# A decoder's opening: parameter rows on a second DMA queue, constants after roots, token mixing folded into the weights

## The chip, the cores and the metric

The kernel runs on one core of a Trainium2 chip. The metric is the device time of one execution in microseconds (us), lower is better. A core has a matrix engine (TensorE, PE in the rows), a vector engine (VectorE, DVE), an activation engine (ScalarE, ACT), a general engine (GpSimd, POOL) and a sync engine (SyncE, SP) whose work here is to issue DMAs. Each engine runs its own instruction list in order, and they meet only at semaphores.

## The reference

Two decoder layers are computed over x (8 sequences of 256 tokens, width 128) with a context of 8 x 512 tokens. Six sublayers follow each other, each followed by a layer norm of x plus the sublayer: a recurrent block (RWKV), memory attention, a top-1 mixture of experts, sparse attention, cross attention, and a top-2 mixture. Only the first matters for this change:

```python
h = layer_norm(x, ln_att_g, ln_att_b)
sx = time_shift(h)                       # h of the token before, 0 ahead of the first
k = (h * att_mix_k + sx * (1.0 - att_mix_k)) @ att_wk
v = (h * att_mix_v + sx * (1.0 - att_mix_v)) @ att_wv
r = sigmoid((h * att_mix_r + sx * (1.0 - att_mix_r)) @ att_wr)
att = r * wkv(att_time_decay, att_time_first, k, v) @ att_wo   # a recurrence over tokens
x = x + att
h = layer_norm(x, ln_ffn_g, ln_ffn_b)
sx = time_shift(h)
kf = square(relu((h * ffn_mix_k + sx * (1.0 - ffn_mix_k)) @ ffn_wk))
rf = sigmoid((h * ffn_mix_r + sx * (1.0 - ffn_mix_r)) @ ffn_wr)
return x + rf * (kf @ ffn_wv)
```

`wkv` keeps a running maximum of the keys that decays by `w` per token, a numerator and a denominator, both scaled by exponentials of differences to that maximum, and divides the one by the other.

## The kernel before

The batch is worked in 4 groups of 2 sequences, 512 tokens each. The recurrent block of group n + 1 is computed inside the last two sublayers of group n, beside their matmuls. For group 0 there is nothing to put it beside: it stands alone at the start, with the loading and turning of the weights. This stretch is called the opening, and the change touches it alone. After it come the four groups.

Everything is ordered by hand: each engine's block is a Python function that emits its instructions in order, and waits are written as `wait_ge(semaphore, count)`. There is no planner.

**The loads.** SyncE issues all DMAs of the opening. First x of group 0, then `rec_loads`: 12 single rows of 128 parameters (layer norm scales, decay, mixes) and 6 blocks of rows into the tile `col_rows`, then wk, wv, wr, wo, fwk, fwv, fwr. Then `loads` (weights of the attentions, 4 of them of 512 KB into the arena's `xw_raw`, and 8 rows for broadcasts), the context, and `layer_loads` (expert weights).

**TensorE** waits for GpSimd's constants (`consts_ready`, line 531) and for all of `rec_loads` (line 532). Then it turns `col_rows` (78 rows) into `cols`, whose columns hold one parameter per partition (`set_up(0)`, line 516), turns the normalised x (line 479), and multiplies the three mixed inputs by wk, wv and wr (line 556). After the wait for `weights_loaded` it turns 8 groups of four 128 x 128 weight blocks and two more weights; then `rec_attend` (the product with wo, line 499), which waits for VectorE's `wkv_ready`; then `qk_fold` (line 518), the sum `xbv_out` (16 instructions, line 523), 8 rows broadcast over the partitions by a matmul with ones (line 527); after all of those have been copied, the turn of the context (line 539), two key projections of 128 x 512 (`project_k`, line 760), the turn of the second normalised input, two value projections (`project_v`, line 766), and the feed forward matmuls (line 567 on). An fp32 product shows as two instructions in the trace.

**ScalarE** copies results out of the accumulator banks (line 1127), applies scale and shift to the turned input (line 1159, tile `hT`), and computes the exponentials (lines 1171, 1173) and the sigmoid (line 1177). In the opening it holds back after `set_up(0)` until `cols_ready` is 6, that is until VectorE has derived five small tables from `cols`.

**GpSimd** first makes all constants: memsets, iotas, selects (line 1461), copies (lines 1473, 1474). Then come the two reciprocal square roots of the first layer norm (`rec_rstd`, lines 1491 and 1493), the two products `b2v` and `bv_` (lines 1534, 1538), the three steps of the numerator `t_num` (lines 1542, 1544, 1549), the roots of the second norm, and the split of the expert bias b1 into three bf16 parts (lines 1624 to 1630).

**VectorE** computes the norm's moments and the normalised x (lines 1652 to 1660), the token change `dT` (line 1684) and the three mixes (line 1690, two instructions each), the running maximum (a scan for each sequence, line 1720), the own maximum (line 1726), four differences (line 1735), the denominator's scans (line 1740) and the numerator's (line 1745), two steps of `t_den` (lines 1752, 1754), reciprocals (line 1758), and the product with GpSimd's numerator (line 1763). This last gives `wkv_ready`.

The listing holds the functions that the diff touches. Names of tiles are reused in the trace: `big` is `ex` or a product, `nT` the keys, `V` the values, `arena` any tile carved from it.

## Time and profile before

| what | value |
|---|---|
| median of 3 runs | 1188.58 us |
| lowest, highest | 1184.47, 1196.2 us |
| the profiled execution | 1197.25 us |
| its span in the trace | 1195.5 us |
| busy: PE, PEld, DVE, ACT, POOL | 1063.4, 661.9, 726.5, 646.6, 186.0 us |

The profiled execution is one run of its own: its time is the span and 1.75 us around it, and it lies 8.67 us above the median of the three runs. Durations of steps come from its trace, so sums are made against 1197.25. PE is the matmul side of TensorE, PEld its loading of weights, which overlaps. The busy time of PE is not PE at its peak, since matmuls are pipelined. Lines such as L1740 are lines of the kernel before.

### The profile page before, as it was taken

The page shows a single profiled execution, that of the slowest core. Times are in us where ns is not written, and L with a number is a line of the kernel's source. Part 1 is how long each engine was busy: PE and PEld are TensorE (multiplying, and loading weights), DVE is VectorE, ACT ScalarE, POOL GpSimd, SP SyncE. Part 2 cuts the span into 40 slices and gives each one's busy share as a digit, 9 for nine tenths or more (in the row PEclk, how much of TensorE's full clock was granted, in tenths as well). Part 3 has the DMA queues.
Part 4 walks back from the last instruction along what each step waited for, and adds up shares of the span by engine and source line. Part 5 has one row for each costly group of instructions (what it writes and reads, how often), then busy time and mean ns, then how long its engine had stood idle before and what let it go on. Part 6 is the DMA issues. An engine that isn't in the chain of part 4 may idle for free.

```text
span 1195.5 us, 23126 instructions
## 1 busy us (share of the span) xinstructions
PE 1063.4 (89%) x8821; PEld 661.9 (55%) x8821; DVE 726.5 (61%) x1827; ACT 646.6 (54%) x1429; POOL 186.0 (16%) x313
## 2 busy tenths in 40 slices
PE   3789988998989998999898998899979999899957
PEld 1664545554766456455586454555567635545546
DVE  5552475888644175788854338488874417567861
ACT  3452356775655054778565235577755605477724
POOL 4320220212120040012102013020212004000000
PEclk9799999999899998999899999999989999899979
DMA  7400000000000000000000000000000000000000
GB/s 221 143 1 1 1 2 4 8 19 2 2 11 1 1 1 1 10 20 2 1 1 11 1 1 1 2 10 19 1 1 10 1 1 1 2 1 2 2 1 10
DMA packets 21072, 15.77 MB, mean 13 GB/s; under 512 B 871, under 2 KB 18644, under 8 KB 20956
## 3 DMA queue, kind: packets, MB, share of 16 engines
q1 hardware_dynamic: 20956, 14.24, 4.0%
q8 instruction: 70, 1.15, 0.4%
q14 instruction: 46, 0.38, 0.1%
HBM read 13.18 MB, written 1.05 MB: 12 GB/s over the span
## 4 chain that ended last, share of the span: by engine, by line
PE 41%; issue 40%; ACT 5%; POOL 5%; DVE 5%; POOLq 1%; DVEq 1%; SPq 1%; DMA 0%; ACTq 0%
PE ps L728 10%; PE ps L908 5%; PE ps L944 4%; PE ps L926 3%; PE ps L760 3%; PE ps L766 3%; POOL rstd L1493 2%; PE ps L757 2%; ACT arena L1328 2%; PE ps L627 1%; PE ps L953 1%; PE ps L741 1%; DVE nmax L1982 1%; ACT arena L1127 1%; PE ps L660 1%
## 5 line engine op out<-in xcount | busy, mean ns | idle before, releaser
L1127 ACT ACTIVATE arena<-ps 128x512 f32<-128x512 f32 (+6 forms) x300 | 162.9, 575 | 146.2 <-PE ps L926 56.2
L1328 ACT ACTIVATE arena<-ps,nmax 128x512 f32<-128x512 f32 x256 | 173.6, 685 | 7.9 <-DVE nmax L1982 4.8
L1982 DVE TENSOR_REDUCE nmax<-ps 128x1 f32<-128x512 f32 x256 | 163.9, 683 | 22.6 <-PE ps L908 22.0
L1987 DVE COPY arena<-ps 128x512 f32<-128x512 f32 x128 | 88.1, 688 | 61.0 <-PE ps L926 61.0
L926 PEld LDWEIGHTS ps<-ident,arena 64*128 64x128 f32 x2048 | 76.6, 138 | 82.7 <-issue 42.2
L728 PE MATMUL ps<-big,w1a 128*128 128x512 f32 x256 | 117.3, 604 | 0.0
L926 PE MATMUL ps<-ident,arena 64*128 64x64 f32 x2048 | 92.4, 228 | 11.7 <-ACT arena L1127 6.3
L1491 POOL TENSOR_TENSOR vare<-mv,eps_ln 128x2 f32<-128x2 f32 x64 | 13.0, 204 | 565.8 <-DVE mv L1655 565.5
L728 PEld LDWEIGHTS ps<-big,w1a 128*128 128x128 f32 x256 | 46.3, 189 | 57.5 <-issue 56.5
L1875 DVE TENSOR_TENSOR big<-XT,ps 128x512 f32<-128x512 f32 x32 | 22.0, 687 | 90.4 <-PE ps L712 90.3
L1991 DVE SCALAR_TENSOR_TENSOR X<-ps,cross_inv,X 128x128 f32<-128x128 f32 x256 | 72.4, 342 | 3.2 <-issue 0.5
L1270 ACT ACTIVATE big<-ps 128x512 f32<-128x512 f32 x16 | 9.6, 597 | 116.1 <-PE ps L728 116.1
L760 PE MATMUL ps<-ctxT,xwT 128*128 128x512 f32 x128 | 68.8, 653 | 0.0
L766 PEld LDWEIGHTS ps<-xwT,ctxT 128*128 128x128 f32 x512 | 62.3, 193 | 8.1 <-issue 7.7
L766 PE MATMUL ps<-xwT,ctxT 128*128 128x128 f32 x512 | 65.0, 278 | 0.0
L1493 POOL TENSOR_TENSOR rstd<-vare,neg_half 128x2 f32<-128x2 f32 x72 | 51.1, 710 | 10.2
L1328 ACT ACTIVATION_READ_ACCUMULATOR arena<-ps,nmax 128x1 f32 x256 | 51.6, 202 | 0.0
L953 PEld LDWEIGHTS ps<-xwT,arena 64*128 64x128 f32 x512 | 31.6, 187 | 20.5 <-DVE arena L1987 16.8
L1915 DVE TENSOR_TENSOR arena<-ps,s_nmax 128x1024 f32<-128x1024 f32 x32 | 39.2, 1225 | 2.4
L1908 DVE TENSOR_REDUCE s_nmax<-ps 128x8 f32<-128x1024 f32 x32 | 38.9, 1216 | 1.9 <-PE ps L818 1.9
L831 PEld LDWEIGHTS ps<-ident,arena 64*128 64x128 f32 x512 | 19.5, 146 | 36.7 <-ACT arena L1291 30.2
L953 PE MATMUL ps<-xwT,arena 64*128 64x128 f32 x512 | 38.0, 285 | 1.9 <-ACT arena L1127 1.9
(376 smaller groups left out, 2035.4 us busy)
## 6 DMA issues: line engine op xcount, KB each, us to landing
ctx<-in_ctx_dram SPq DMA_DIRECT2D x4, 512.0 KB, 3.9
w1a<-in_L_ffn_W_dram SPq DMA_DIRECT2D x1, 2048.0 KB, 9.6
w1b<-in_L_ffn_W_dram SPq DMA_DIRECT2D x1, 2048.0 KB, 11.6
w2b<-in_L_ffn_W_dram SPq DMA_DIRECT2D x8, 256.0 KB, 6.9
X<-in_x_dram SPq DMA_DIRECT2D x4, 256.0 KB, 2.8
out_dram<-Y SPq DMA_DIRECT2D x4, 256.0 KB, 2.3
arena<-in_L_xattn_Wq_dram SPq DMA_DIRECT2D x1, 512.0 KB
arena<-in_L_xattn_Wk_dram SPq DMA_DIRECT2D x1, 512.0 KB
```

What stands on the lines that cost most here:

```text
L728: last = pe.matmul(bank(acc[h]), w1a[:, e, h * P:(h + 1) * P], XE[:, e % 2, :], start=(e == 0), stop=(e == E - 1))
L760: pe.matmul(bank(b), xwT[:, 1, j, :], ctxT[:, seq * CTX:(seq + 1) * CTX], start=True, stop=True)\
L766: last = pe.matmul(ps[:, b, k * P:(k + 1) * P], ctxT[:, c * P:(c + 1) * P], xwT[:, 2, j, :], start=True, stop=True)
L908: pe.matmul(bank(2 * (t % 2) + h), QTs[r, j % 2, t * P:(t + 1) * P], keys_of(j, t // QT)[r, :], start=True, stop=True).then_inc(c_ps, 1)
L926: last = pe.transpose(ps[:, 4 + u, o:o + DK], cprob[r, 2 * (t % 2) + h, k * P:(k + 1) * P], ident[r, r])
L953: last = pe.matmul(ps[:, b + h, t * D:(t + 1) * D], CTs[r, j % 2, t * P:(t + 1) * P], xwT[r, 3, j, :], start=True, stop=True)
L1127: return act.activation(dst, src, ACT.Copy)
L1328: act.activation(cprob[:, 2 * (t % 2) + h, :], bank(2 * (t % 2) + h), ACT.Exp, bias=nmax[:, s:s + 1], accum_out=rsum[:, j % 2, s:s + 1]).t ...
L1493: return pool.tensor_tensor(result[:, r], with_eps[:, r], neg_half[:, r], ALU.pow)
L1982: dve.tensor_reduce(nmax[:, s:s + 1], bank(s % 4), AX.X, ALU.max, negate=True)\
L1987: dve.tensor_copy(cprobT[:, 2 * (t % 2), :], bank(4)).then_inc(cT_even, 1)
L1991: last = dve.scalar_tensor_tensor(out=X1[:, t, :], in0=ps[:, b, t * D:(t + 1) * D], scalar=cross_inv[:, j % 2, 2 * t + h:2 * t + h + 1], i ...
```

## The change

- The 12 single parameter rows (`first_rows`) are issued by ScalarE's queue; SyncE issues x, then wk, wv, wr (`mix_loads`), then the rest as before. TensorE's first work waits for the identity matrix and the 12 rows alone.
- GpSimd makes the identity and the small constants first, signals `ident_ready`, makes some more, then does the first norm's roots. The masks come after the roots, the head constants after the numerator, the expert rows (`pick`) after the second norm's roots; `consts_ready` is awaited at the end of the opening.
- `col_rows` is turned in two parts: the 12 rows first, all else later as `set_up(1)`.
- The token change and the three mixes of the opening are gone. VectorE splits each weight instead, `own = w * mix` and `past = w - own`, and TensorE forms h @ own + sx @ past: two products instead of one. The keys are computed a sequence at a time, and ScalarE's copies and VectorE's scans too.
- ScalarE no longer waits for `cols_ready` 6 ahead of `hT`; that wait now stands before the turned context. Three of the five small tables are made after `wkv_ready`.
- VectorE computes `b2v` and `bv_`; GpSimd waits for `den_ready`, the finished denominator, and then computes the three steps of the numerator.
- `qk_fold` comes before `rec_attend`; the broadcast rows before `xbv_out`; the second turn after one key projection instead of two.
- In the four groups no instruction changes.

```diff
-            pe.wait_ge(consts_ready, 1)
-            pe.wait_ge(rec_loaded, 16 * len(rec_loads))
+            pe.wait_ge(ident_ready, 1)
+            pe.wait_ge(rows_loaded, 16 * len(first_rows))
             set_up(0)
...
+            def first_turn():
+                pe.wait_ge(xhat_ready, 1)
+                turn_seq(NHAT, 5, 0).then_inc(half_turned, 1)
+                pe.wait_ge(xhat_ready, 2)
+                turn_seq(NHAT, 4, 1).then_inc(hT_ps, 1)
+
+            def first_keys(seq):
+                if seq == 0:
+                    pe.wait_ge(half_ready, 1)
+                    pe.wait_ge(mix_ready, 1)
+                else:
+                    pe.wait_ge(hT_ready, 1)
+                o = ps[:, 6 + seq, seq * SEQ:(seq + 1) * SEQ]
+                pe.matmul(o, own_w[0], hT[:, seq, 1:SEQ + 1], start=True, stop=False)
+                return pe.matmul(o, past_w[0], hT[:, seq, 0:SEQ], start=False, stop=True)
+
+            def first_project(w, b):
+                pe.wait_ge(vr_mix_ready, w)
+                pe.matmul(bank(b), own_w[w], hT[:, :, 1:SEQ + 1], start=True, stop=False)
+                pe.matmul(bank(b), past_w[w], hT[:, :, 0:SEQ], start=False, stop=True).then_inc(kvr_ps, 1)
+
             def first_recurrent(n):
-                rec_turn(n, 1, 5)
-                rec_project(n, 0, 6)
-                rec_project(n, 1, 7)
-                rec_project(n, 2, 5)
+                first_turn()
+                first_keys(0).then_inc(half_key_ps, 1)
+                first_keys(1).then_inc(kvr_ps, 1)
+                first_project(1, 5)
+                first_project(2, 4)
+                pe.wait_ge(rec_loaded, 16 * len(rec_loads))
+                set_up(1)
 
                 pe.wait_ge(weights_loaded, 16 * len(loads))
-                for i in range(1, N_TURNS):
+                for i in range(2, N_TURNS + 1):
                     set_up(i)
                 rec_attend(n)
-                for i in range(N_TURNS, N_SETUP):
+                for i in range(N_TURNS + 1, N_SETUP):
                     set_up(i)
                 pe.wait_ge(wT_sb, N_SETUP)
                 turn_ctx(n, 2)
-                for seq in range(GROUP):
-                    pe.wait_ge(ctxT_ready, n * 2 + seq + 1)
-                    project_k(5, seq, seq)
+                pe.wait_ge(ctxT_ready, n * 2 + 1)
+                project_k(5, 0, 0)
                 rec_turn(n, 2, 5)
+                pe.wait_ge(ctxT_ready, n * 2 + 2)
+                project_k(5, 1, 1)
                 for seq in range(GROUP):
                     project_v(5, 2 + seq, seq)
                 for h in range(HT):
@@ -605,6 +638,7 @@
                 rec_gate(n)
                 rec_narrow(n, 0)
                 rec_narrow(n, 1)
+                pe.wait_ge(consts_ready, 1)
 
...
+            for dst, src in first_rows:
+                act.dma_start(dst, src).then_inc(rows_loaded, 16)
             set_up(0)
             act.wait_ge(wT_sb, 1)
             act.activation(decay_e[:, :], col(R_DECAY), ACT.Exp).then_inc(cols_ready, 1)
-            act.wait_ge(cols_ready, 6)
...
             def first_recurrent(n):
-                rec_turned(n, 1, 5, R_LNG, R_LNB)
-                rec_projected(n, 0, 6)
-                rec_projected(n, 1, 7)
-                for i in range(4):
-                    rec_exp(n, i)
-                rec_receptance(n, 5)
+                act.wait_ge(half_turned, 1)
+                first_turned(0).then_inc(half_ready, 1)
+                act.wait_ge(hT_ps, 1)
+                first_turned(1).then_inc(hT_ready, 1)
+                act.wait_ge(half_key_ps, 1)
+                first_key(0).then_inc(half_key_ready, 1)
+                act.wait_ge(kvr_ps, 1)
+                first_key(1).then_inc(kvr_ready, 1)
+                rec_exp(n, 0)
+                rec_exp(n, 1)
+                rec_projected(n, 1, 5)
+                rec_exp(n, 2)
+                rec_exp(n, 3)
+                rec_receptance(n, 4)
                 for i in range(1, N_SETUP):
                     set_up(i)
+                act.wait_ge(cols_ready, 6)
                 ctx_turned(n, 2)
-                for seq in range(GROUP):
-                    keys(n, 5, seq, seq)
+                keys(n, 5, 0, 0)
                 rec_turned(n, 2, 5, R_FLNG, R_FLNB)
+                keys(n, 5, 1, 1)
                 for seq in range(GROUP):
                     context_values(n, 5, 2 + seq, seq)
```

On GpSimd and VectorE (bodies of `masks`, `head_constants` and `expert_rows` are the old instructions, regrouped):

```diff
             pool.memset(ident[:, :], 0.0)
-            pool.memset(causal_f[:, :], 0.0)
...
             pool.memset(neg_half[:, :], -0.5)
             pool.memset(eps_ln[:, :], 1e-5)
             pool.memset(eps_rms[:, :], 1e-6)
             pool.memset(eps_post[:, :], 1e-12)
+            pool.memset(ones[:, :], 1.0)
+            pool.drain()
+            select(ident[:, :], ALU.not_equal, 1.0, 0, [[-1, P]], 1)
+            pool.drain().then_inc(ident_ready, 1)
+            pool.memset(causal_f[:, :], 0.0)
+            pool.memset(before_f[:, :], 1.0)
...
@@ -1613,11 +1672,13 @@
                 rstd_of(it, 6, eps_ln)
 
             rec_rstd(0, 1)
-            rec_weighted_values(0)
-            rec_own_values(0)
+            masks()
+            pool.wait_ge(den_ready, 1)
             rec_numerator(0)
             rec_numerator_gated(0)
+            head_constants()
             rec_rstd(0, 2)
+            expert_rows()
 
             pool.wait_ge(b1_loaded, 16)
...
+            def mixed_weights(w, row, done):
+                dve.tensor_scalar(own_w[w], (wk, wv, wr)[w][:, :], col(row), None, ALU.mult)
+                dve.drain()
+                dve.tensor_tensor(past_w[w], (wk, wv, wr)[w][:, :], own_w[w], ALU.subtract).then_inc(done, 1)
+
+            def first_difference(i, a, b):
+                dve.tensor_tensor(ex[i][:, :, :], a, b, ALU.subtract).then_inc(wkv_arg, 1)
+
+            def first_max(b):
+                return dve.tensor_tensor_scan(o_max[:, b, 1:SEQ + 1], w_bc[:, :], kS[:, b, :], -1e38, ALU.add, ALU.max)
+
+            def first_columns():
+                dve.wait_ge(cols_ready, 1)
+                dve.wait_ge(mix_loaded, 16 * len(mix_loads))
+                mixed_weights(0, R_MK, mix_ready)
+                dve.tensor_scalar(decay_w[:, :], decay_e[:, :], -1.0, None, ALU.mult).then_inc(cols_ready, 1)
+                mixed_weights(1, R_MV, vr_mix_ready)
+                dve.tensor_scalar(w_bc[:, :], w_bc[:, :], decay_w[:, 0:1], None, ALU.add).then_inc(cols_ready, 1)
+                mixed_weights(2, R_MR, vr_mix_ready)
...
+            def first_recurrent(n):
+                dve.wait_ge(half_key_ready, 1)
+                first_max(0)
+                dve.wait_ge(kvr_ready, 1)
+                first_max(1).then_inc(o_max_ready, 1)
+                dve.drain()
+                first_difference(0, o_max[:, :, 0:SEQ], o_max[:, :, 1:SEQ + 1])
+                first_difference(1, kS[:, :, :], o_max[:, :, 1:SEQ + 1])
                 rec_first_max()
                 dve.drain()
-                rec_differences()
+                first_difference(2, o_max[:, :, 0:SEQ], o_new[:, :, :])
+                first_difference(3, kS[:, :, :], o_new[:, :, :])
                 rec_key_sum(n)
+                dve.wait_ge(kvr_ready, 2)
+                dve.tensor_tensor(b2v[:, :, :], ex[1][:, :, :], vS[:, :, :], ALU.mult).then_inc(b2v_ready, 1)
                 rec_value_sum(n)
+                dve.wait_ge(wkv_exp, 4)
+                dve.tensor_tensor(bv_[:, :, :], ex[3][:, :, :], vS[:, :, :], ALU.mult)
                 rec_denominator(n)
+                dve.drain().then_inc(den_ready, 1)
                 for b in range(GROUP):
                     rec_inverse(b)
                 rec_wkv(n)
+                other_columns()
                 rec_second_norm(n)
                 rec_feed_mix(n)
                 rec_feed(n)
```

## Rows read from the trace of the kernel before

**Rows 1.** The page: the span, and the chain that ended last, by engine.

```profile
span 1195.5 us, 23126 instructions
...
PE 41%; issue 40%; ACT 5%; POOL 5%; DVE 5%; POOLq 1%; DVEq 1%; SPq 1%; DMA 0%; ACTq 0%
...
```

**Rows 2.** Windows: stretch, busy us (count) by engine, granted clock, DMA, GB/s.

```profile
...
66.00:1195.00 1129.00, 1026.56 (x8645) 634.80 (x8643) 689.00 (x1741) 621.75 (x1376) 158.68 (x244) 0.97 0.02 4
28.40:31.50 3.10, 2.88 (x14) 2.88 (x15) 3.01 (x4) 2.74 (x7) 1.43 (x2) 0.51 1.10 350
35.40:42.00 6.60, 4.41 (x20) 4.41 (x21) 3.99 (x10) 0.28 (x1) 0.52 (x2) 0.50 1.21 296
45.50:48.50 3.00, 3.00 (x10) 1.73 (x8) 0.00 (x0) 1.20 (x2) 2.59 (x4) 0.50 0.00 0
...
```

**Rows 3.** Chain of waits, opening: start, duration (us), what was waited for.

```profile
...
9.75 3.05 DMA fwr<-in_L_attn_ffn_wr_dram
...
13.84 0.15 DVE decay_w L2148
...
17.83 2.09 PE ps L556 x2
...
```

**Rows 4.** Timeline of SyncE's DMA issues: start, duration (us), destination, source.

```profile
...
0.82 0.45 SPq L440 DMA_DIRECT2D X<-in_x_dram  x1
...
4.68 0.25 SPq L451 DMA_DIRECT2D col_rows<-in_L_xattn_norm_w_dram  x1
...
18.63 0.25 SPq L453 DMA_DIRECT2D arena<-in_L_ffn_br_dram  x1
...
25.59 13.65 SPq L457 DMA_DIRECT2D w2b<-in_L_ffn_W_dram  x8
...
```

**Rows 5.** Timeline of VectorE, opening; in brackets idle time before, releaser.

```profile
...
10.50 0.60 DVE L1660 TENSOR_SCALAR NHAT<-X,mv,rstd 128x128 f32<-128x128 f32 x2 [5.39 <-POOL rstd L1493]
...
20.57 1.27 DVE L1720 TENSOR_TENSOR_SCAN o_max<-w_bc,nT 128x256 f32<-128x256 f32 x2 [1.22 <-ACT nT L1127]
...
25.33 3.36 DVE L1740 TENSOR_TENSOR_SCAN q_den<-big 128x256 f32<-128x256 f32 x2
...
29.95 1.71 DVE L1752 TENSOR_TENSOR big<-big,q_den 128x512 f32<-128x512 f32 x1
...
33.41 3.36 DVE L1758 RECIPROCAL alpha<-big 128x256 f32<-128x256 f32 x2
...
43.67 0.85 DVE L1660 TENSOR_SCALAR NHAT<-X,mv,rstd 128x128 f32<-128x128 f32 x2 [0.66 <-POOL rstd L1493]
...
```

**Rows 6.** Timeline of GpSimd, opening.

```profile
...
9.41 0.19 POOL L1491 TENSOR_TENSOR vare<-mv,eps_ln 128x2 f32<-128x2 f32 x1
...
24.96 1.57 POOL L1534 TENSOR_TENSOR big<-big,V 128x512 f32<-128x512 f32 x1 [13.50 <-ACT big L1173]
...
```

**Rows 7.** Timeline of TensorE, opening.

```profile
...
22.83 1.97 PE L516 MATMUL ps<-ident,arena 128*128 128x128 f32 x16 [0.30 <-DMA arena<-in_L_ffn_br_dram]
...
37.59 2.08 PE L499 MATMUL ps<-wo,alpha 128*128 128x128 f32 x8 [5.19 <-DVE alpha L1763]
...
49.95 1.95 PE L766 MATMUL ps<-xwT,ctxT 128*128 128x128 f32 x16
52.81 3.70 PE L567 MATMUL ps<-qT,fwk 128*128 128x512 f32 x8 [0.91 <-DVE qT L1690]
...
61.60 1.88 PE L760 MATMUL ps<-ctxT,xwT 128*128 128x512 f32 x4
...
```

**Rows 8.** Groups by form, VectorE after 60 us: count, busy us, mean ns.

```profile
...
L1752 DVE TENSOR_TENSOR big<-big,q_den 128x512 f32<-128x512 f32 x3 | 2.1, 693 | 0.5 <-issue 0.5
...
```

**Rows 9.** Groups by form, GpSimd after 60 us; idle before.

```profile
...
L1549 POOL TENSOR_TENSOR big<-big,OT 128x512 f32<-128x512 f32 x3 | 3.8, 1266 | 11.4 <-ACT OT L1177 11.4
...
```

**Rows 10.** Timeline of ScalarE, opening.

```profile
...
26.18 1.28 ACT L1177 ACT_TABLE_LOAD   x1
...
27.97 3.25 ACT L1127 ACTIVATE xwT<-ps 128x512 f32<-128x512 f32 x6
...
```

137 lines of the change are left out of this document (67 added, 70 removed).

## The prediction

> **What bounds the kernel now.** I read the page first, then windows of the opening, then the chain of waits, then each engine's timeline. The page's chain belongs to TensorE and to issue time [rows 1]. After 66 us TensorE is busy 1026.56 of 1129.00 us at a granted clock of 0.97, and no instruction of that stretch changes [rows 2]. So what the opening loses or gains arrives at the end nearly one for one, and the rest stays as it is. The other windows of [rows 2] matter for the clock: three stretches stood at 0.5 (1.2 of 2.4 GHz).
>
> In the opening the chain of waits goes from SyncE's list of DMA issues to the landing of fwr at 12.80, by the small tables to the first mix, and to the key product at 17.83 [rows 3]. After it VectorE is the chain, up to the product that releases TensorE at 37.59. From there TensorE leads, until the feed forward at 52.81 and the first layer's end.
>
> **The change part by part.** All sums are against this execution, 1197.25 us with 1195.5 us of span.
>
> Start of the key product. x is issued at 0.82 and the last single row at 4.68; with x's 0.45 taken off, the 12 rows cost about 0.3 each [rows 4]. ScalarE can start its own list when SyncE does, so its last issue begins at 0.82 + 11 x 0.3 = 4.1. A load with others ahead of it took 3.05 from issue to landing (fwr, [rows 3]), so the rows are there at 7.2 at the latest; a little less is likely for 0.5 KB, I take 7.0. From landing to VectorE's first small table took 1.04 (12.80 to 13.84); 12 columns instead of 78 make it 0.9. The split of wk is one scalar product and one subtraction on 128 x 128, about 0.7 with the drain. The first key product starts at 8.6 instead of 17.83: **-9.2** (ends: -9.6, rows at 6.6; -6.7, issues at twice the price on that queue).
> What could be later is the normalised x. VectorE had its moments ready at 10.50 - 5.39 = 5.11 and waited for GpSimd's roots, which stood behind the constants until 9.41 [rows 5, 6]. A root takes 1.09 from its start to x (9.41 to 10.50). With fewer constants ahead it follows the moments: x is there at 6.2 and 7.2, beside the wait for the rows, and costs nothing. If GpSimd got to it only at 7, the second half would come at 9.1 and hold the second key product alone, which starts later than that.
>
> Keys. Before, product, copy and both scans took 17.83 to 20.57 + 1.27 = 21.84, so 4.0. The product was two instructions of 512 columns in 2.09, and the same form took 1.88 / 4 = 0.47 each at 61.60 [rows 7]: it ran at half speed though the record there shows no lower clock. Now there are eight of 256 columns, as long as four of 512: 4 x 0.95 = 3.8. The first half's copy and scan lie beside the second half's product, the second half's cost 1.1. 4.9 against 4.0: **+0.9** (ends: -1.0 at full speed; +1.5).
> The doubled products for v and r are needed only by `b2v` and by the numerator's last step; 2 x 3.8 after the keys end at about 21, beside VectorE's maximum and differences. `b2v` needs only v, at 16.
>
> From the scans to the reciprocals. The denominator's two scans took 3.36, the same form 1.27 [rows 5], the first with GpSimd's product of 1.57 beside it [rows 6]: -2.1. The two steps of `t_den` took from 29.95 to 33.41, 3.46, beside the numerator; alone such a step takes 0.69 [rows 8], 1.5 with drains: -1.9. VectorE takes over `b2v` and `bv_`, 2 x 0.69: +1.4. Two more waits: +0.2. Together **-2.4** (ends -1.6 and -2.8).
> The rows show VectorE slowed by 2.1 and 1.9 beside GpSimd's products; the numerator beside the reciprocals is the price to watch. The Trainium skill (SBUF — State Buffer, "Who interferes with whom") says that the two engines share one pair of ports exclusively, a VectorE operation with two SBUF inputs against a GpSimd one that reads; by it the reciprocals, with one input, are free. The trace agrees as far as it goes: 3.36 for two, next to GpSimd's last step.
>
> Numerator. All three steps now start after the denominator, beside the reciprocals (3.36). Alone a step took 1.27 [rows 9], three with drains 4.1 and the semaphore 0.1; at 1.57 each 5.0. So the product waits 0.8 to 1.7 more than before; I take **+0.9**.
>
> Masks. GpSimd makes them from about 7 on, beside VectorE's splits. NHAT beside a GpSimd cast took 0.85 where the same pair took 0.60 [rows 5]. Two or three such hits: **+0.2** (0 to +0.9).
>
> The release of TensorE (T) thus moves by -9.2 + 0.9 - 2.4 + 0.9 + 0.2 = -9.6, from 37.59 to 28.0. Is all else there by then? The last small row was issued at 18.63 and TensorE waited for it until 22.83 [rows 4, 7]. 12 issues leave SyncE's list, 3.6: landing at 19.2. ScalarE's table load of 1.28 before the sigmoid and then the weight copies, 3.25 for six [rows 10], ten copies 5.2: done at 25. The cover is 3 us. Were the loads bound by transfer, not issue, they would land at 22.83 and the copies end at 28.2: +0.2. `qk_fold` slips into this gap, two of L499's eight at 2.08: **-0.4** (0 to -0.5) [rows 7].
>
> Second turn. One projection, two instructions of 512 columns (0.94), moves behind the turn. TensorE was idle for 0.91 before 52.81, after value projections of 1.95 [rows 7]; the chain turn, ScalarE, VectorE now begins 0.94 earlier and TensorE has 2.9 of work under it. Gain 0.9 at most. But GpSimd's expert rows and split of b1 now lie beside VectorE's change and mixes, all of two inputs; the scans lost 2.1 to such a neighbour. **0** (-0.9 to +1.2).
>
> Clock. Before, TensorE was idle 5.19 ahead of 37.59 and the clock stood at 0.50 from 35.4 to 42.0, with 4.41 us of work: half of it, 2.2, is lost; from 45.5 to 48.5 another 1.5. At 28.4 to 31.5 the clock was low too, after an idle stretch, and rose while TensorE only turned weights [rows 2]. Now the idle gap before T is 3 at most, perhaps 2, with the turned weights right before it. Either the clock holds (-2.2) or it doesn't; and the weak work of the broadcast rows now lies just before `xbv_out`, so a low stretch after it costs up to +1.5. **-0.8**.
>
> Sum: -9.6 (to T) - 0.4 + 0 - 0.8 = **-10.8**. The profiled time becomes 1186.4. The median of the runs stands 8.67 below the profiled one, so I forecast 1188.58 - 10.8 = **1177.8 us**, 0.91% less.
>
> **The rivals.** What a measurement can tell from no change is about 1%, 11.9 us.
>
> *The clock holds through the opening.* -2.2 in place of -0.8, no block at the second turn (-0.9), the keys partly at full speed (-0.8): -10.8 - 1.4 - 0.9 - 0.8 = -13.9, with some of it -12. Time 1174.7 to 1176.6. For: the shorter gap. Against: the key product ran at half speed and its idle lead-in stays.
>
> *GpSimd's moved work blocks VectorE.* Numerator +1.7, masks +0.9, second turn +1.2: 2.7 more than forecast, -8.1: 1180.5. For: NHAT's 0.85, the scans' 3.36. Against: much of it is small, on 8 partitions.
> By the rule of the Trainium skill named above this would be the way it goes, for the split of b1 reads SBUF throughout.
>
> *The rows land late.* Both queues feed the same engines; at twice the price of an issue the last begins at 7.4, the key product at 12: -7.5, so 1181.
>
> *The expected gain isn't there*, because a later load or wait ends last. The expert weights were issued until 39.24 [rows 4], and no load of the opening is on the chain after 22.83. I see no such wait.
>
> *Slower.* One mechanism: ScalarE's queue comes under back-pressure. SyncE's eight issues of w2b took 13.65, 1.7 each [rows 4]. At that price the 12 rows begin their last issue at 19.5 and land at 22.5, 15.5 later than forecast: -10.8 + 15.5 = +4.7, 1193. It decides from 1.3 per issue on, and the kernel is slower by over 1% from 2.4 on (22.7 / 11 more than 0.3). Against: it came behind megabytes in the queue, and here only x and small weights are under way.
>
> **How the numbers follow.** Forecast, -9 to -12: 0.48, of which 0.07 lies beyond 1%. Clock holds, -12 to -14: 0.32. GpSimd blocks: 0.08. Rows late: 0.04. No gain: 0.02. Slower: 0.06, of which 0.04 by over 1%. So faster by over 1%: 0.07 + 0.32 = 0.39; within 1%: 0.41 + 0.08 + 0.04 + 0.02 + 0.02 = 0.57; slower: 0.04. The likeliest time is 1177.8. The range reaches from the clock's case, 1174.7, to the late rows, 1181, and gets 4 more at each end because medians stray (three runs lie between 1184.47 and 1196.2): 1171 to 1185. It leaves out the slower case, no gain, and the tails.
>
> **What would show it.** The wait for the 12 rows ends at 7.0 and the first key instruction starts at 8.6; later by more than 1 means the queue. The denominator's scans take 1.27, each `t_den` step 0.69; more means GpSimd is still beside them. GpSimd's three steps end 0.9 after the reciprocals. T is at 28.0. The set-up copies end before T, or the loads did not move up. The second mixes at the feed forward take 0.48 each, or b1's split is in their way. The granted clock around T is 1.0 in the rival and 0.5 in the forecast's worse half. The stretch after the first layer lasts as long as before. The forecast is wrong if T lies above 31, or if the later groups change their length by over 3 us.

## The result and the profile after

The changed kernel takes 1178.14 us (median of 15 runs, 1176.0 to 1188.04), the kernel before 1190.68 us (median of 15, 1184.47 to 1197.71). The ratio is 0.9894, with a 95% interval of [0.9872, 0.9915]: 12.5 us or 1.06% less. The forecast was 1177.8. Its size was 10.8; the kernel before came out 2.1 higher than in the first three runs, so part of the agreement of the two absolute times is luck: the change is worth 1.7 more than forecast, and the kernel that it is taken from is 2.1 slower.

The profiled execution after took 1182.05 us, with a span of 1180.1. So it is 15.2 us shorter than the one before [rows 1], and both lie above their medians. The page after, the chain by engine (before: [rows 1]):

```profile
...
issue 42%; PE 41%; POOL 6%; ACT 5%; DVE 4%; POOLq 2%; DVEq 1%; ACTq 0%; DMA 0%
...
```

TensorE still owns the end; the share of SP's queue is gone from the chain. Windows of the kernel after, with columns as in [rows 2] (behind the counts of the five engines stands the granted clock):

```profile
...
17.70:24.30 6.60, 5.60 (x26) 5.60 (x27) 6.25 (x8) 4.58 (x9) 2.45 (x2) 0.51 0.99 336
24.70:42.00 17.30, 14.89 (x90) 11.02 (x89) 11.74 (x26) 9.30 (x25) 13.35 (x27) 1.00 0.96 284
...
```

One stretch of low clock is left, while the weights are turned; from 24.7 on the clock stood at 1.0 where before two more stretches were at 0.5 [rows 2]. Now the timeline of TensorE after (start, duration; in brackets the idle time before it and what ended it):

```profile
...
6.79 0.25 PE L524 MATMUL ps<-ident,col_rows 12*128 12x12 f32 x1 [6.79 <-DMA col_rows<-in_L_xattn_norm_w_dram]
...
8.40 1.19 PE L604 MATMUL ps<-hT,kv_more 128*128 128x256 f32 x2 [0.32 <-ACT hT L1223]
...
11.04 0.59 PE L605 MATMUL ps<-hT,kv_more 128*128 128x256 f32 x2
...
18.70 6.59 PE L524 MATMUL ps<-ident,arena 128*128 128x128 f32 x32 [3.56 <-DMA arena<-in_L_ffn_br_dram]
...
26.49 1.16 PE L507 MATMUL ps<-wo,alpha 128*128 128x128 f32 x8 [0.46 <-DVE alpha L1813]
...
38.76 3.70 PE L575 MATMUL ps<-qT,fwk 128*128 128x512 f32 x8 [1.26 <-DVE qT L1751]
...
43.87 3.84 PE L587 MATMUL ps<-fwv,big 128*128 128x128 f32 x32 [0.52 <-DVE big L1832]
...
```

The 12 rows are there at 6.79, the keys start at 8.40 instead of 17.83, the weights land at 18.70 instead of 22.83, and T, the release of TensorE, comes at 26.49 instead of 37.59 [rows 3, 7]. The idle time ahead of it fell from 5.19 to 0.46 in this execution. VectorE and GpSimd after:

```profile
...
5.59 0.60 DVE L1721 TENSOR_SCALAR NHAT<-X,mv,rstd 128x128 f32<-128x128 f32 x2 [0.48 <-POOL rstd L1552]
...
12.09 0.69 DVE L1854 TENSOR_TENSOR_SCAN o_max<-w_bc,nT 128x256 f32<-128x256 f32 x1 [0.50 <-ACT nT L1161]
...
16.26 1.27 DVE L1790 TENSOR_TENSOR_SCAN q_den<-big 128x256 f32<-128x256 f32 x2
...
20.08 0.69 DVE L1802 TENSOR_TENSOR big<-big,q_den 128x512 f32<-128x512 f32 x1
...
21.70 3.37 DVE L1808 RECIPROCAL alpha<-big 128x256 f32<-128x256 f32 x2 [0.16 <-issue]
25.75 0.69 DVE L1813 TENSOR_TENSOR alpha<-alpha,big 128x512 f32<-128x512 f32 x1 [0.68 <-POOL big L1608]
...
36.63 2.08 DVE L1751 SCALAR_TENSOR_TENSOR qT<-O,cols,hT 128x256 f32<-128x256 f32 x2
38.63 2.23 DVE L1751 SCALAR_TENSOR_TENSOR qpT<-O,cols,hT 128x256 f32<-128x256 f32 x2
...
```

```profile
...
4.50 0.20 POOL L1550 TENSOR_TENSOR vare<-mv,eps_ln 128x2 f32<-128x2 f32 x1 [1.48 <-DVE mv L1716]
...
24.44 1.27 POOL L1608 TENSOR_TENSOR big<-big,OT 128x512 f32<-128x512 f32 x1
...
36.16 1.51 POOL L1689 TENSOR_TENSOR arena<-arena 8x512 f32<-8x512 f32 x1
...
```

The denominator's scans take 1.27 instead of 3.36 and the first step of `t_den` 0.69 instead of 1.71 [rows 5]. The reciprocals keep their 3.37 with GpSimd's three steps beside them, and the product waits 0.68 for the last of these. Where GpSimd splits b1, the two mixes at the feed forward (two instructions each) take 2.08 and 2.23; alone such a mix takes 0.88.

**A second profile of each.** Both kernels were profiled once more, unchanged, in the last two experiments. In the tables below "first key" is the start of the first key product, "scans" the end of the maximum's two scans, "T" the start of the product with wo, "output" the start of the first feed forward output product (L579 before, L587 after).

| profile | first key | scans | reciprocals | T | output | span less output |
|---|---|---|---|---|---|---|
| before | 17.83 | 21.84 | 33.41 | 37.59 | 57.92 | 1137.6 |
| before, again | 18.66 | 22.68 | 34.24 | 38.42 | 58.53 | 1129.5 |
| after | 8.40 | 12.78 | 21.70 | 26.49 | 43.87 | 1136.2 |
| after, again | 8.56 | 13.47 | 22.39 | 27.16 | 48.72 | 1127.6 |

T repeats within 0.83 us for the same kernel, and moved by 11.1 and 11.3. What follows it does not repeat: 17.38 and 21.56 us from T to the output product for one and the same program, and 8 us more or less in the stretch after it.

### The profile page after: what moved, and what is told of

The parts are those of the page before. It is cut to its first block, busy times and chain, and to the rows that moved or that the text cites. A ratio compares the mean times of both kernels' runs of the same rounds, so it can differ in the third digit from the quotient of the medians.

```text
span 1180.1 us, 23157 instructions
## 1 busy us (share of the span) xinstructions
PE 1062.5 (90%) x8832; PEld 661.6 (56%) x8832; DVE 724.9 (61%) x1828; ACT 647.2 (55%) x1432; POOL 183.9 (16%) x311
## 2 busy tenths in 40 slices
DMA packets 21069, 15.74 MB, mean 13 GB/s; under 512 B 871, under 2 KB 18644, under 8 KB 20956
## 4 chain that ended last, share of the span: by engine, by line
issue 42%; PE 41%; POOL 6%; ACT 5%; DVE 4%; POOLq 2%; DVEq 1%; ACTq 0%; DMA 0%
PE ps L762 10%; PE ps L942 5%; PE ps L978 4%; PE ps L960 3%; PE ps L800 3%; PE ps L794 3%; POOL rstd L1552 2%; PE ps L791 2%; ACT arena L1379 2%; PE ps L987 1%; PE ps L775 1%; DVE nmax L2067 1%; PE ps L661 1%; ACT arena L1161 1%; POOLq L1551 1%
## 5 line engine op out<-in xcount | busy, mean ns | idle before, releaser
L865 PEld LDWEIGHTS ps<-ident,arena 64*128 64x128 f32 x512 | 19.2, 143 | 36.7 <-ACT arena L1342 30.1
```

## The experiments

My theory was the forecast's: T moves by the sum of its terms, and the total moves with T. The rivals that were left after the result: that the clock gives a part of the gain, that the second queue gives nothing, and that b1's split takes something back at the feed forward. Ten kernels change a part, two repeat a kernel unchanged; line numbers in their rows are their own.

### Rows issued by SyncE

```diff
-            for dst, src in first_rows:
-                act.dma_start(dst, src).then_inc(rows_loaded, 16)
...
             load_x(0)
+            for dst, src in first_rows:
+                sp.dma_start(dst, src).then_inc(rows_loaded, 16)
             for dst, src in mix_loads:
```

> The changed kernel, but SyncE issues the 12 single rows, after x and before wk, wv and wr, as before the change. Landmarks of the changed kernel: first key instruction at 8.40, release of TensorE by VectorE's last product (T) at 26.49, first feed forward output product at 43.87. If the second queue earns by its issue time (my theory): the rows land near 7.2 instead of 6.65, wk, wv and wr land 12 x 0.3 = 3.6 later, at 8 to 9, so the split of wk and the first key instruction come at 9 to 10; the loads for the weight turns land at 22.3 instead of 18.7, the turns (7 us) and copies end near 29.5 and T's work starts there, 3 later than now; output product at 46.5 to 47.5. If only the narrower wait earned (TensorE waits for 12 rows, not for all): first key instruction within 0.7 of 8.4 and T within 1 of 26.5.

Measured: 1177.52 us in one run, T 28.42, output 45.69: between the two cases that I had set out. TensorE and VectorE in its opening:

```profile
...
6.00 0.25 PE L526 MATMUL ps<-ident,col_rows 12*128 12x12 f32 x1 [6.00 <-DMA col_rows<-in_L_xattn_norm_w_dram]
...
22.19 5.54 PE L526 MATMUL ps<-ident,arena 128*128 128x128 f32 x32 [6.26 <-DMA arena<-in_L_ffn_br_dram]
...
28.42 1.06 PE L509 MATMUL ps<-wo,alpha 128*128 128x128 f32 x8
...
```

```profile
...
26.50 0.69 DVE L1813 TENSOR_TENSOR alpha<-alpha,big 128x512 f32<-128x512 f32 x1 [0.68 <-POOL big L1608]
...
```

The rows came earlier (6.00), not later. The wk, wv and wr behind them came later, but their split ended in time: first key 8.63, only 0.2 behind. What the 12 issues cost is the landing of the weights, 22.19 instead of 18.70. VectorE's product was done at 27.19, and TensorE, still with the turned weights and the fold of qk, came to it at 28.42. T is 1.3 to 1.9 later than in the two profiles of the kernel after. So ScalarE's queue is worth 1.2 us here (28.42 less 27.19), and through the later weights; VectorE's path gains 0.2 of it at most. The rest of the 1.9 lies mostly in the second half of the keys, which ran at half speed here as in the second profile of the kernel after.

### The roots behind all constants

```diff
-            rec_rstd(0, 1)
             masks()
+            head_constants()
+            expert_rows()
+            rec_rstd(0, 1)
             pool.wait_ge(den_ready, 1)
```

> The changed kernel, but GpSimd makes all its constants (masks, head constants, expert rows) before the first two roots. My prediction held that the roots must come early or the normalised x is late: roots at 9.4, x at 10.5 and 11.5, first key instruction at 12 instead of 8.40, T at 30 instead of 26.49. Rival: the rows and the split of the weights hold the keys anyway, and T moves by under 1. The output product then starts at 47 to 47.5 (theory) or below 45 (rival).

Measured: 1182.85 us in one run; first key 14.03, scans 18.81, T 32.49. GpSimd, and then TensorE:

```profile
...
10.29 0.18 POOL L1550 TENSOR_TENSOR vare<-mv,eps_ln 128x2 f32<-128x2 f32 x1
...
```

```profile
...
32.49 2.08 PE L507 MATMUL ps<-wo,alpha 128*128 128x128 f32 x8 [3.36 <-DVE alpha L1813]
...
```

The root starts 5.8 later and T is 5.3 to 6.0 later than in the two profiles of the kernel after. I had expected 3.5. VectorE's list splits wk only behind both halves of x, and the second half was normalised at 13.32, so the first key came at 14.03 and not at 12. This is the largest single part. The roots are worth it only since the 12 rows no longer hold the keys: before, the first half of x was normalised at 11.10 and TensorE's first work waited for fwr until 12.80 [rows 3, 5].

### The products and the numerator on GpSimd, as before

```diff
-            pool.wait_ge(den_ready, 1)
+            pool.wait_ge(kvr_ready, 2)
+            rec_weighted_values(0)
+            rec_own_values(0)
             rec_numerator(0)
...
-                dve.tensor_tensor(b2v[:, :, :], ex[1][:, :, :], vS[:, :, :], ALU.mult).then_inc(b2v_ready, 1)
...
-                dve.tensor_tensor(bv_[:, :, :], ex[3][:, :, :], vS[:, :, :], ALU.mult)
```

> The changed kernel, but GpSimd computes b2v, bv_ and the numerator as soon as their inputs are there, beside VectorE's sums, as before the change. Theory of the shared ports: the denominator's two scans take about 3.4 instead of 1.27 and the two t_den steps 3.4 instead of 1.5; VectorE is spared 1.35 for the two products and the numerator no longer trails the reciprocals (0.7): T later by 2 to 2.5, at 28.5 to 29. Rival, that VectorE was slow for another reason of the old order (the four differences, the exponentials on ScalarE): scans stay at 1.27, T is 1.5 to 2 earlier by VectorE, and held at 26 by the copies of the turned weights.

Measured: 1188.07 us in one run; scans 13.44, T 29.20. VectorE:

```profile
...
18.00 1.26 DVE L1792 TENSOR_TENSOR_SCAN q_den<-big 128x256 f32<-128x256 f32 x2
19.18 2.27 DVE L1797 TENSOR_TENSOR_SCAN p_num<-big 128x256 f32<-128x256 f32 x2
21.55 1.71 DVE L1804 TENSOR_TENSOR big<-big,q_den 128x512 f32<-128x512 f32 x1
...
```

The `q_den` scans, for which I had expected 3.4, escaped GpSimd's product here: it started at 16.07 and met the last difference instead (1.75 against 0.68). `p_num`'s scans and the steps of `t_den` did not escape (2.27, 1.71 and 1.61). The stretch from the scans to T is the number that repeats best. It lasts 15.75 and 15.74 in the two profiles of the kernel before and 15.76 here; with the products on VectorE it lasts 13.71 and 13.69 in the two after, 13.68 with the late roots and 13.70 with mixed inputs (below). So this part is worth 2.05 us at T, where the forecast had 1.5 (-2.4 + 0.9). (The kernel with the rows on SyncE is left out: TensorE and not VectorE sets its T.)

### Inputs mixed, weights not split

> The changed kernel, but the weights are not split: VectorE computes the token change and the three mixes of the inputs (0.69 + 3 x 0.88) and TensorE multiplies once, the keys still by sequence. Theory: hT is complete at 8.72, change and key mix end at 10.4, so the keys start 2 later, but take half as long (1.9 instead of 3.2); then the v and r mixes hold VectorE until 12.2. Maximum's end 13.5 to 14 instead of 12.78; T 27.2 to 27.8 instead of 26.49: the split earns about 1. Rival: it earns the whole time of change and mix, 1.6 to 2.4, and T is above 28.

```diff
-                mixed_weights(0, R_MK, mix_ready)
...
-                mixed_weights(1, R_MV, vr_mix_ready)
...
-                mixed_weights(2, R_MR, vr_mix_ready)
+                dve.wait_ge(hT_ready, 1)
+                token_change()
+                token_shift(zk, R_MK, mix_ready)
+                token_shift(zv, R_MV, vr_mix_ready)
+                token_shift(zr, R_MR, vr_mix_ready)
```

TensorE has one product for each of k, v and r again. Measured: 1177.92 us in one run; first key 10.75, scans 13.97, T 27.67. TensorE:

```profile
...
10.75 2.08 PE L601 MATMUL ps<-qT,wk 128*128 128x256 f32 x4 [2.36 <-DVE qT L1747]
...
```

The first key is 2.2 to 2.4 later, but with one product instead of two the keys take 3.2 instead of 4.4 to 4.9. What the split weights bring at T is 0.5 to 1.2.

### TensorE kept busy ahead of T, in the kernel before

```diff
                 for i in range(1, N_TURNS):
                     set_up(i)
+                for _ in range(5):
+                    pe.matmul(bank(6), wk[:, :], zk[:, :, :], start=True, stop=True)
                 rec_attend(n)
```

> The kernel before, with five products of 128 x 512 into a free bank put between the last turned weight and the product with wo: TensorE stays busy from 32.4 until 36.8 instead of idling 5.19; the five results are not used. Clock theory: from the release by VectorE's last product (T, 37.59) to the first feed forward output product took 20.33 there and 17.38 in the changed kernel, because the clock stood at 0.5 after the idle stretch. Here the granted clock stays at 1.0 around T, the product with wo takes 1.05 instead of 2.08, and the distance falls to 17.5 to 18.8 with T unchanged; the whole kernel gains 1.5 to 3. Rival, that the new order (broadcast rows first, second turn sooner) made the 17.38: the distance stays at 20.3 and the time is the same.

Measured: 1192.34 us median of 10 runs, ratio to before 0.9997 [0.9965, 1.0029]. The profiled execution:

```profile
...
31.68 5.17 PE L593 MATMUL ps<-qT,wk 128*128 128x512 f32 x10
37.42 1.16 PE L499 MATMUL ps<-wo,alpha 128*128 128x128 f32 x8 [0.57 <-DVE alpha L1765]
...
55.62 3.84 PE L579 MATMUL ps<-fwv,big 128*128 128x128 f32 x32 [0.52 <-DVE big L1784]
...
```

The clock held: the product with wo took 1.16 instead of 2.08 [rows 7], and T to output took 18.20 instead of 20.33. The opening is 2.3 to 2.9 shorter than in the two profiles of before, and the median of the total did not fall. But the interval reaches from 4.2 us less to 3.5 us more: it holds the whole gain of 2.3 to 2.9 as well as none. This run shows what the clock does to the opening, and leaves open whether the gain arrives at the end.

### b1 split behind the mixes

```diff
             expert_rows()
+            pool.wait_ge(mix_ready, 3)
 
             pool.wait_ge(b1_loaded, 16)
```

> The changed kernel, but GpSimd begins the split of b1 only after VectorE's last mix of the second turn. In the changed kernel the first mix took 2.09 instead of 0.88 and TensorE idled 1.26 ahead of the feed forward. Port theory: the change and mixes take 0.69 and 0.88 each, the feed forward starts right behind the value projections, at 37.6 to 37.8 instead of 38.76, output product at 42.7 to 42.9 instead of 43.87: the kernel gains 1.1. Rival: the mixes were slow for ScalarE's copies or the projections' reads; nothing moves.

Measured: 1179.06 us median of 8, ratio 0.9906 [0.9872, 0.994]. VectorE and TensorE at the feed forward:

```profile
...
36.47 0.88 DVE L1752 SCALAR_TENSOR_TENSOR qT<-O,cols,hT 128x256 f32<-128x256 f32 x2
...
39.19 4.60 DVE L1833 TENSOR_TENSOR big<-big 128x512 f32<-128x512 f32 x4 [1.05 <-ACT big L1216]
...
```

```profile
...
37.40 3.70 PE L575 MATMUL ps<-qT,fwk 128*128 128x512 f32 x8
...
43.84 5.46 PE L587 MATMUL ps<-fwv,big 128*128 128x128 f32 x32 [1.85 <-DVE big L1833]
49.14 1.88 PE L794 MATMUL ps<-ctxT,xwT 128*128 128x512 f32 x4
...
```

The mixes are free again (0.88) and the feed forward starts 1.36 sooner, without a wait. But now the split lies beside the squares, which need 4.60 for four, and the output product starts at 43.84 as in the kernel after. It then takes 5.46 instead of 3.84: TensorE had been idle for 1.85 and its granted clock was 0.69 on average from 43.84 to 49.30. The next projection starts at 49.14, in the kernel after at 47.55. So the cost was moved, not removed, and in this profile the late split loses 1.6 behind the landmark that I measured by.

### The second turn behind both key projections

> The changed kernel, but both key projections stand ahead of the second turn, as before the change. Forecast of the changed kernel: the sooner turn earns 0.9 unless GpSimd's split of b1 eats it; TensorE idled 1.26 behind it, so VectorE's chain is the bound there. Theory: turn, mixes and feed forward all come 0.9 later, from T to the output product 18.3 instead of 17.4 at the same clock. Rival: VectorE's mixes then fall past the split of b1, run at 0.88, and 0.5 or more of the 0.9 comes back.

```diff
                 project_k(5, 0, 0)
-                rec_turn(n, 2, 5)
                 pe.wait_ge(ctxT_ready, n * 2 + 2)
                 project_k(5, 1, 1)
+                rec_turn(n, 2, 5)
```

ScalarE's list follows it. Measured: 1187.27 us in one run; T 26.91. The feed forward:

```profile
...
42.02 5.40 PE L575 MATMUL ps<-qT,fwk 128*128 128x512 f32 x8 [2.53 <-DVE qT L1751]
...
```

The idle time ahead of it is 2.53 us instead of 1.26 (1.17 in the second profile of the kernel after). So the sooner turn is worth some 1.3, where I had said 0. It is one execution, and VectorE's change and first mix lay beside the split of b1 here too (1.13 and 2.07), while the second mix took 0.87. (Another 1.6 of the delay is the sum xbv_out at low clock, 3.61 instead of 2.05.)

### Unused products and the rows ahead of T

> The changed kernel, with b1's split late, four unused products of 128 x 512 while TensorE waits for the weight loads (14.9 to 18.7 there, with 3.56 idle), and the eight broadcast rows ahead of the product with wo. Clock theory: the 32 turns of weights, 6.59 at a clock of 0.5, take 4.5 to 5 and ScalarE's copies end by 24.5; the rows fit in before T at 26.5 or hold it to 26.7; T to output product falls from 17.38 to 14.4 (rows 1.9, split 1.1), so output product at 41 instead of 43.87 and the kernel gains 2.5 to 3 over the changed one. Rival: the turns stay at 6.6 (their rate is ScalarE's), rows end at 28 and T's work starts there: gain 1.1 to 1.5.

```diff
                 set_up(1)
+                pe.wait_ge(kvr_ready, 1)
+                for _ in range(4):
+                    pe.matmul(bank(6), own_w[0], hT[:, :, 1:SEQ + 1], start=True, stop=True)
...
-                for i in range(2, N_TURNS + 1):
+                for i in range(2, N_SETUP - 1):
                     set_up(i)
                 rec_attend(n)
```

This is on top of the late split. Measured: 1177.73 us median of 12 (1173.04 to 1185.84), ratio 0.9915 [0.9881, 0.9949]. The turns took 3.71 instead of 6.59, all at full clock, and then:

```profile
...
23.81 2.30 PE L535 MATMUL ps<-arena,ones 1*128 1x128 f32 x16
26.70 2.07 PE L507 MATMUL ps<-wo,alpha 128*128 128x128 f32 x8 [0.59 <-DVE alpha L1817]
28.57 3.62 PE L531 MATMUL ps<-xwT,arena 128*128 128x128 f32 x16
...
```

The clock that was won in the turns was lost right after, with only 0.59 of idle time ahead of T. My rule "a short gap keeps the clock" does not hold as such. The broadcast rows multiply a single row, and they and short gaps came before the fall. The output product starts at 44.67, where I had expected 41, and takes 5.47: it waits for the squares beside b1's split, as with the late split alone.

### b1 split sooner, expert rows last

```diff
-            head_constants()
-            rec_rstd(0, 2)
-            expert_rows()
-
             pool.wait_ge(b1_loaded, 16)
...
+            bias_split(b1_parts[0:E, :])
+            rec_rstd(0, 2)
+            head_constants()
+            bias_split(b1_mid[:, :])
+            pool.tensor_copy(b1_low[:, :], b1_rest).then_inc(b1_split, 1)
+            expert_rows()
```

> The kernel after, with GpSimd's list reordered: numerator, first half of the split of b1, roots of the second norm, head constants, second half of the split, expert rows (pick) last. The split's two subtractions with two inputs then no longer lie beside VectorE's change and mixes at 35.8 to 40.8; only casts, a memset and a select do. If GpSimd's operations with two inputs are what slows the mixes (2.08 and 2.23, alone 0.88 each): the feed forward (line 575 of after) starts at 37.4 instead of 38.76, the squares take their 0.7 each, the output product starts at 42.4 instead of 43.87, and T stays within 0.3 of 26.49. If any neighbour on GpSimd slows them, one-input casts too: mixes above 1.5 each and no gain. A risk: the first half of the split lies ahead of the second norm's roots (before at 29.08) and could make them late by up to 0.5. Total: 1.4 less on average than the kernel after, which the spread of single runs hides.

Measured: 1180.27 us median of 6 (1176.49 to 1187.75), ratio 0.9899 [0.9853, 0.9945]. T 27.47, output 46.88, with the clock at 0.5 from 30 to 36. VectorE, and what GpSimd did beside it:

```profile
...
26.36 1.06 DVE L1816 TENSOR_TENSOR alpha<-alpha,big 128x512 f32<-128x512 f32 x1 [0.68 <-POOL big L1608]
...
40.22 1.49 DVE L1754 SCALAR_TENSOR_TENSOR qT<-O,cols,hT 128x256 f32<-128x256 f32 x2
41.64 0.87 DVE L1754 SCALAR_TENSOR_TENSOR qpT<-O,cols,hT 128x256 f32<-128x256 f32 x2
...
```

```profile
...
26.26 0.60 POOL L1681 CAST b_parts<-arena 8x512 bf16<-8x512 f32 x1
...
39.73 1.30 POOL L1545 CAST pick<-arena 8x1024 bf16<-8x1024 f32 x1
...
```

The mixes cost 1.49 + 0.87 instead of 2.08 + 2.23, but this does not show what the new order is worth. The second turn came later here, with the low clock, and in the second profile of the kernel after, where it came later too, the old order had 1.07 + 0.87 behind a change of 1.62 (here 0.79, alone 0.69). By that profile the new order gains 0.4. Casts on 8 partitions are felt too: the last product, with a cast beside it, took 1.06 instead of 0.69 and put T 0.37 later. The Trainium skill (SBUF — State Buffer, "Who interferes with whom") has it so: a VectorE instruction with two SBUF inputs contends with a GpSimd instruction that reads SBUF. The trace agrees for a cast as for a subtraction.

### TensorE busy throughout

```diff
+            pe.wait_ge(zeros_ready, 1)
+            for _ in range(6):
+                pe.matmul(ps[:, 7, 0:SEQ], w_bc[:, 0:P], w_bc[:, :], start=True, stop=True)
             pe.wait_ge(ident_ready, 1)
...
+                for _ in range(3):
+                    pe.matmul(bank(6), own_w[0], hT[:, :, 1:SEQ + 1], start=True, stop=True)
                 rec_attend(n)
```

This is on top of the kernel with the split sooner (the last one), and has the 4 unused products after the keys as well, which the cut above leaves out.

> As the one with the split sooner, and TensorE is given products whose result is not used: 6 of 256 columns from 1.4 us on (on zeroes, before the parameter rows land), 4 of 512 columns in the wait for the weights, 3 ahead of the product with wo. The output stays the reference's. If the low clock costs what I say: key products at full clock take about 0.5 instead of 1.0 each, the maximum's scans end at 11.5 instead of 12.8, T comes at 25.3 instead of 26.5, the product with wo takes 1.16 and the sum xbv_out 1.95, and the output product starts at 41.0 to 41.5. If TensorE's half speed in the keys has another cause (first use of its inputs, fp32): keys stay near 1.0 each and T at 26.4. The low stretches after the opening may fall either way, so the total says little: 1174 to 1180.

Measured: 1178.92 us median of 6 (1172.7 to 1180.24), ratio 0.9867 [0.9829, 0.9905].

```profile
...
9.08 0.59 PE L608 MATMUL ps<-hT,kv_more 128*128 128x256 f32 x2
...
25.75 1.16 PE L507 MATMUL ps<-wo,alpha 128*128 128x128 f32 x8
...
42.17 3.84 PE L590 MATMUL ps<-fwv,big 128*128 128x128 f32 x32 [0.59 <-DVE big L1843]
...
```

The landmarks moved as the clock theory says, though T came 0.5 and the output product at least 0.7 later than I had expected. A key product takes 0.59 instead of 1.06, the scans end at 11.68, T is at 25.75 and the output product at 42.17, the earliest of all. So what TensorE did beforehand sets the keys' speed, and neither fp32 nor a first use of the inputs does. That it is the clock is inferred, for the record of the kernel after shows 1.00 during its slow keys:

```profile
...
9.00:12.00 3.00, 3.00 (x10) 2.30 (x9) 1.32 (x4) 0.71 (x2) 0.00 (x0) 1.00 0.79 220
...
```

The total is not below that of the kernel after, run beside it (1177.25). How much it should have been below is not sharp: the opening is 6.5 shorter than in that kernel's second profile, and 1.7 shorter than in its first. Against the kernel that it is built on (1180.27) it is 1.4 less in the median, with an opening 4.7 shorter. All these differences are within what medians of six stray. Two windows show one place where it went, the first of this kernel and the second of the kernel after in its second profile, both some 96 us behind the output product:

```profile
...
138.00:146.00 8.00, 8.00 (x50) 3.09 (x48) 5.95 (x9) 3.94 (x4) 2.70 (x3) 0.50 0.01 2
...
```

```profile
...
144.00:152.00 8.00, 7.09 (x124) 4.24 (x124) 7.55 (x11) 5.58 (x7) 3.24 (x3) 1.00 0.01 2
...
```

The clock stood at 0.50 in the one and at 1.00 in the other, with TensorE busy for 8.00 and 7.09 of the 8 us; they are not the same instructions in full, so their counts are not compared.

The granted clock of every run says more than the medians. Span times what is missing to full clock was 29.3 to 38.9 us in the six runs of the busy kernel, 35.9 on average, and 34.1 to 35.3 in the six of the kernel after, 34.5 on average. In the profiles the opening's share of this, up to the output product, is 0.0 in the busy kernel; in the kernel after it is 3.4 in the first and 6.8 in the second. So, as far as six runs tell, what the opening no longer lost was lost behind it.

### The kernel after, again

> The kernel after, unchanged, on the same chip as its two variants, for the direct comparison: median 1176 to 1180, ratio to before 0.989, landmarks within 0.3 us of the first profile (first key product 8.4, T 26.5, output product 43.9); what differs between this profile and the first lies in the low-clock stretches after the opening.

Measured: 1177.25 us median of 6 (1176.12 to 1178.66), ratio to before 0.9865 [0.983, 0.99]. T 27.16, 0.7 later than before where I had allowed 0.3, and the output product at 48.72 and not 43.9; there my expectation failed. TensorE, and VectorE at the feed forward:

```profile
...
18.57 5.38 PE L524 MATMUL ps<-ident,arena 128*128 128x128 f32 x32 [2.43 <-DMA arena<-in_L_ffn_br_dram]
...
27.16 2.08 PE L507 MATMUL ps<-wo,alpha 128*128 128x128 f32 x8 [2.47 <-DVE alpha L1813]
...
32.67 3.78 PE L531 MATMUL ps<-xwT,arena 128*128 128x128 f32 x16
...
```

```profile
...
40.78 1.62 DVE L1745 TENSOR_TENSOR O<-hT 128x512 f32<-128x512 f32 x1 [6.78 <-ACT hT L1194]
...
```

The clock rose sooner in the turns (5.38 instead of 6.59), TensorE was idle for 2.47 and the clock fell around T. This execution has the longer opening by 4.85 us and is still 3.8 us shorter as a whole. The Trainium skill (TensorE: Matmul & The Clock Gate, Part 1) notes, for the start of a kernel, that the same kernel shows a different number of matmuls at the low clock from run to run. The two profiles agree, also behind the start: the same 32 turns took 6.59 and 5.38. With the later turn the split of b1 met VectorE's change (1.62) and hardly the mixes (1.07 and 0.87), so the 2.08 and 2.23 of the first profile are not a fixed price.

### The kernel before, again

> The kernel before, unchanged, for a second look at its opening. The second look at the kernel after repeated every step that ends at VectorE within 0.7 us (T 27.16 against 26.49), but its clock was low from 27 to 37 where the first had 1.0. If the same holds here: first key product 17.8 and T 37.6, each within 0.7, while the stretch from T to the output product (20.33 in the first look) may lie anywhere between 17.5 (clock held) and 22. If T itself moves by over 1, then the comparison of T between variants rests on too little.

Measured: 1189.77 us in one run; first key 18.66, T 38.42, output 58.53. T moved by 0.83, past the 0.7 expected and inside the bound of 1; the wait for fwr ended 0.85 later (13.78). From T to the output product it was 20.11, close to the first profile. TensorE:

```profile
...
38.42 2.07 PE L499 MATMUL ps<-wo,alpha 128*128 128x128 f32 x8 [5.42 <-DVE alpha L1763]
...
```

This run is 7.5 us shorter than the first profile of the same kernel, with an opening that is 0.6 longer: all of it lies behind the opening.

## Why the prediction was right, and where not

**Start of the keys (-9.2).** Measured -9.4 and -10.1. The rows ended their wait at 6.79 and 7.02 (7.0 forecast); the issues on ScalarE's queue cost what they cost on SyncE's, so neither the late rows nor the slower case came. The normalised x was there when I said. (The forecast priced the late rows twice: -6.7 as the end of this term, and a key product at 12, which is -5.8, in the rival.)

**Keys (+0.9).** Measured +0.4 and +0.9, by whether the clock rose during the second half. The half speed that I read out of 2.09 against 0.47 was real: with TensorE busy beforehand a key product took 0.59 and the stretch from first key to scans 3.1 instead of 4.4 to 4.9. The doubled products for v and r ran at full speed already: they ended at 15.07 where I had about 21, which nothing waited for.

**Scans to reciprocals (-2.4).** 11.57 became 8.92: -2.65. The scans took the 1.27 and the steps the 0.69 named; the waits cost less than 0.2.

**Numerator (+0.9).** Measured +0.6: 4.18 from the reciprocals to T became 4.79. The three steps took 1.19, 1.27 and 1.27, hardly more than alone, and the reciprocals did not slow (3.37 against 3.36).

**Masks (+0.2).** VectorE's first scan waited for ScalarE, not for a split: 0.

**T.** Forecast -9.6 to 28.0, measured -11.1 and -11.3. Every term erred to the same side, by 0 to 0.9; none failed.

**Cover of the copies (3 us).** Wrong in the first profile: the set-up copies ended at 26.4, some 0.1 before T. I had the landing right (19.2 against 18.70), but not that TensorE would turn the weights at the low clock, 6.59. In the second, with 5.38 for the turns, the copies ended at 25.04, 2.1 before T. A faster VectorE path would have run into this, as the rows on SyncE did, where T waited for TensorE.

**Second turn (0).** The block by b1's split was real (2.08 and 2.23 in the first profile, 1.62 for the change in the second), and the sooner turn was still worth some 1.3. Without the block the feed forward starts 1.36 sooner, but the squares take the gain.

**Clock (-0.8).** Not settled. In the first profile the stretch from T to the output product was 2.95 shorter than before, in the second 1.45 longer, for the same program. The forecast treated time at the low clock in the opening as lost for the end. This is doubtful, and not refuted. The busy kernel speaks against it: its opening lost nothing to the clock, and its runs lost as much in all as those of the kernel after (35.9 and 34.5 us on average). The kernel before kept busy (opening 2.3 to 2.9 shorter, ratio 0.9997) and the two profiles after (opening 4.85 longer, span 3.8 shorter) fit that, but single executions and medians stray by as much.

**The rest stays as it is.** On average it does. In single executions the stretch behind the output product lasted 1127.6 to 1137.6, with no difference in its instructions. I summed its time at less than full clock, weighted by what was missing, in windows of 2 us: 28.0 us in the second profile after, 30.9 in the second before, 38.3 in the first of both, 39.0 in the busy kernel. Taken off, 1097.0 to 1099.6 are left. So nearly all the difference in the rest is clock. One of the pieces is the stretch shown above, at half clock from some 94 us behind the output product on, present in the busy kernel and in the one with the sooner split, and in none of the four profiles of the two kernels. The forecast's mark, "over 3 us" in the later groups, was set too fine: one kernel alone moves by 8.

**The sum.** Of the 12.5 us, T carries 11.1 to 11.3. The 1.2 to 1.4 left would be the fold of qk (0.4) and the rest of the turn and of the clock; this was not shown, and it is within the interval of the measurement (10.1 to 15.2 us). By parts, undone one at a time, T moves by 5.3 to 6.0 (roots), 2.05 (products), 0.5 to 1.2 (split weights) and 1.2 (second queue). That makes 9.1 to 10.5, if parts undone one at a time may be added. The shorter list of rows ahead of the first product, and the waits that go with it, were not undone alone.

**Chances.** The likeliest case came true in its mechanism, but not in its size: -12.5 lies outside its -9 to -12, just past the 1% that I had put at 0.39. I had given -12 to -14 to the rival "clock holds", at 0.32; it came by T instead, with the clock held around T in one profile and low in the other. The range held by the sum for T; that the time lies within 0.4 of the forecast is luck.

## What to carry to other kernels

When a chain of vector work releases the matmul engine, read the same form alone and beside its neighbour: the difference (3.36 against 1.27, 1.71 against 0.69) is what a move off the other engine is worth, and here the instructions took just that afterwards. Measure such an edit at the landmark it moves, in two executions, before believing a difference of a few microseconds in the total, and look at the next step too: the late split kept its landmark and lost 1.6 right behind it. Don't count on time won from the low clock in one stretch to arrive at the end: here 2 to 6 us of it in the opening moved the total by nothing that could be told, with intervals of some 4 us to either side.

## What the hardware did that I had not expected

- The clock's low stretches in the later groups come and go between executions of one program, and make 8 us of 1180 (1127.6 against 1136.2 behind the same output product). Whether a shift of the opening chooses among them was not shown.
- The record showed a granted clock of 1.0 during the first key products while they ran at half the speed (1.06 against 0.59 per 256-column pair). What a product takes is the surer sign. That the difference is the clock is inferred: the unused products ahead of the keys were the only thing there that changed for TensorE.
- Even GpSimd's work on 8 of 128 partitions slows VectorE: a cast of 0.60 and the start of the next cost a product 0.37, a subtraction of 1.51 and the cast after it cost a mix 1.20 (2.08 against 0.88).
- Twelve issues of 0.27 us with 0.03 between them cost nearly the same on both queues (0.25 and 0.04 on SyncE's). From SyncE's the rows landed 0.8 to 1.0 sooner, though the last was issued 0.4 later: from the start of its issue TensorE waited 1.3 us there and 2.5 on ScalarE's, beside which SyncE was issuing wk, wv and wr. The cause was not tested.
